# A graph network on one core: four reorderings around the graph stage, the last encoder layer and the decoder's end

## What is computed

```
agg(h) = segment_sum(h[src], dst)                   # the same edges throughout
h = relu(layernorm(x)*g+b @ W1 + b1) @ W2 + b2      # 1024 -> 512 -> 256
3 times: z = relu((h + agg(h)) @ Wa + ba) @ Wb + bb
         h = h + relu(layernorm(z)*g+b)             # encoder, width 256
delta = relu(h @ Wd1 + bd1) @ Wd2 + bd2             # decoder, 256 -> 512 -> 1024
x1 = layernorm(x + layernorm(x + delta)*g+b)
h1 = relu(x1 @ Ws0 + mean(x1) @ Wn0 + b0)           # sage, mean(v) = agg(v)/max(degree,1)
out = layernorm(x1 + h1 @ Ws1 + mean(h1) @ Wn1 + b1)
```

## Time and profile before

| | |
|---|---|
| median of three runs | 1071.99 us (1071.13 to 1073.99) |
| profiled execution, own time | 1074.08 us |
| profiled execution, span | 1072.3 us |
| mean granted clock of TensorE | 0.975 |
| TensorE busy | 1002.2 us, 93% |
| VectorE, ScalarE, GpSimd busy | 536.6, 351.5, 263.8 us |

### The profile page before, as it was taken

One profiled execution on the slowest core, in us unless ns is written; L12 is line 12 of the kernel. 1 busy time (PEld: TensorE's weight loads), 2 busy tenths in 40 slices (PEclk: granted clock), 3 DMA queues, 4 the chain that ended last, 5 costly groups with the idle time before them and its releaser, 6 DMA issues.

```text
span 1072.3 us, 14807 instructions
## 1 busy us (share of the span) xinstructions
PE 1002.2 (93%) x4862; PEld 812.9 (76%) x4862; DVE 536.6 (50%) x1314; ACT 351.5 (33%) x632; POOL 263.8 (25%) x320
## 2 busy tenths in 40 slices
PE   4779899989897898999999999999999999999996
PEld 2367678878787687887777777778887777877774
DVE  7978974374658887333223332222234333334545
ACT  5545552152526477321111221113341011222221
POOL 3000003741416330735004324005206003300000
PEclk9698999999998999999999999999999999999999
DMA  9296344893003584414223104243325335103444
GB/s 327 67 220 186 49 64 89 195 204 84 2 20 109 188 281 150 144 32 138 100 100 102 45 20 160 67 141 128 108 87 166 120 97 164 46 1 121 154 133 133
DMA packets 48263, 127.13 MB, mean 119 GB/s; under 512 B 17775, under 2 KB 18784, under 8 KB 48016
## 3 DMA queue, kind: packets, MB, share of 16 engines
q1 hardware_dynamic: 33622, 74.91, 23.8%
q0 software_dynamic: 8288, 37.29, 12.9%
q10 hardware_dynamic: 6298, 14.21, 3.9%
HBM read 101.76 MB, written 45.13 MB: 137 GB/s over the span
## 4 chain that ended last, share of the span: by engine, by line
PE 83%; DVE 7%; ACT 3%; issue 3%; DMA 2%; POOL 1%; SPq 0%; ACTq 0%; DVEq 0%; POOLq 0%
PE bank L1724 42%; PE bank L1745 17%; PE bank L622 5%; PE bank L1071 5%; PE bank L1103 4%; PE bank L1431 4%; PE bank L586 3%; DMA x_rows<-x 1%; DVE wide L957 1%; PE bank L1412 1%; DVE wide L959 1%; PE bank L1445 1%; ACT xt_f L257 1%; DMA w_f<-W_pairs 1%; PE bank L579 0%
## 5 line engine op out<-in xcount | busy, mean ns | idle before, releaser
L1665 DVE TENSOR_TENSOR h_stage<-h_turned,h_stage 128x1000 fp32r<-128x1000 f32 x80 | 105.5, 1320 | 370.2 <-ACT h_stage L1597 370.2
L1724 PE MATMUL bank<-w_neigh,h_stage 128*125 128x512 f32 x960 | 227.2, 397 | 3.4 <-issue 3.4
L1724 PE MATMUL bank<-w_self,h_stage 128*125 128x512 f32 x960 | 230.3, 395 | 0.0
L1724 PEld LDWEIGHTS bank<-w_neigh,h_stage 128*125 128x125 f32 x960 | 178.2, 187 | 47.3 <-issue 3.6
L1724 PEld LDWEIGHTS bank<-w_self,h_stage 128*125 128x125 f32 x960 | 178.0, 186 | 45.6
L1745 PE MATMUL bank<-g_rows,a_stage 125*125 125x512 f32 x800 | 192.4, 395 | 0.0
L1597 ACT ACTIVATE h_stage<-h_turned 128x1000 fp32r (+1 forms) x80 | 83.8, 1049 | 305.9 <-PE bank L1724 293.5
L1745 PEld LDWEIGHTS bank<-g_rows,a_stage 125*125 125x125 f32 x800 | 148.4, 186 | 37.4
L1562 POOL CAST w_self<-w_stage 128x512 fp32r<-128x512 f32 x32 | 22.7, 711 | 230.2 <-PE bank L1724 221.9
L1103 PE MATMUL bank<-a_turned,gn 125*128 125x418 f32 x360 | 70.5, 354 | 2.8 <-DVE gn L963 2.8
L1103 PEld LDWEIGHTS bank<-a_turned,gn 125*128 125x128 f32 x360 | 67.0, 188 | 4.2 <-DVE gn L963 3.4
(11 more groups left out here) (210 smaller groups left out, 1125.6 us busy)
## 6 DMA issues: line engine op xcount, KB each, us to landing
a_stage<-at_dram SPq DMA_DIRECT2D x40, 625.0 KB, 4.1
w_stage<-w_self POOLq DMA_DIRECT2D x32, 256.0 KB, 3.2
at_dram<-a_turned SPq DMA_DIRECT2D x10, 625.0 KB, 10.5
w_stage<-w_neigh POOLq DMA_DIRECT2D x24, 256.0 KB, 2.9
dec_y<-x_bd SPq DMA_DIRECT2D x10, 512.0 KB, 4.0
dec_x<-x_ob SPq DMA_DIRECT2D x10, 512.0 KB, 4.8
x_dram<-h_rows SPq DMA_DIRECT2D x10, 512.0 KB, 3.0
h_dram<-o ACTq DMA_DIRECT2D x20, 256.0 KB
```

The lines of the kernel that those rows point to most:

```text
L1665: dve.tensor_tensor(st[u][:, 1, :, :], ht[:, :, bass.ds(t * NT, NT)], raw(st[u][:, 0, :, :]), ALU.subtract).then_inc(st_ready, 1)
L1724: mm = pe.matmul(out, st[u][:, a, k, :], w[:, b, k * 512:(k + 1) * 512], start=(k == 0 and p == 0), stop=(k == KD - 1 and p == 2))
```

## The change

1. **Copies of x.** The three pieces are issued in pairs 2, 3 and 4 in place of 0, 1 and 2, still ahead of that pair's `add_eye`.
2. **GpSimd held back.** Before it splits the unit `UNIT_B0` it waits until the degrees are reduced. Behind the layers it waits until all rows of h of the last layer are split, before it forms the low parts of Wd2.
3. **Rows of h.** In the last layer VectorE splits the rows of h of tiles 6 to 9 ahead of the first four products of z1, not behind them.
4. **First h tile.** The decoder's loops end one tile earlier. ScalarE and VectorE do tile 8 in the sage block with the same operations in the same order, except that ScalarE rounds the first tile of h_turned between `roots` and `normalize` of tile 8. `h_stage0` and `h_stage1` change places in memory, so that only the second stage needs the waits for `wn_split` and `x1_read`. TensorE waits for `wn_split` itself.

```diff
@@ -369,8 +369,9 @@
 
         pool.memset(raw(s.at_[:, :, N:NW]), 0.0).then_inc(padded, 1)
         for p in range(PAIRS):
-            own = slice(p * CH, min((p + 1) * CH, N + 128 - NT))
-            for to in ("x_bd", "x_ob") if p < NCH else ():
+            piece = p - (PAIRS - NCH)
+            own = slice(piece * CH, min((piece + 1) * CH, N + 128 - NT))
+            for to in ("x_bd", "x_ob") if piece >= 0 else ():
                 pool.dma_start(io[to][own, :], io["x"][own, :]).then_inc(s.x_copied, 16)
             add_eye(p)
         pool.wait_ge(z1_split, 1)
@@ -830,6 +831,8 @@
 
             if FREED[n]:
                 pool.wait_ge(w_free, FREED[n])
+            if n == UNIT_B0:
+                pool.wait_ge(deg_summed, 1)
             halves(n, SLOT[n])
         pool.wait_ge(s.x_copied, 16 * 2 * NCH)
         for t in range(T):
@@ -837,6 +840,7 @@
                 pool.dma_start(io[to][t * NT:(t + 1) * NT, :], io[row].to_broadcast([NT, D]), accum_op=ALU.add)\
                     .then_inc(x_summed, 16)
         over_layers(pool, layer)
+        pool.wait_ge(h_ready, T * LAYERS)
         for k in range(KH):
 
             hi, lo = [s.w_self[:, h, k * D:(k + 1) * D] for h in range(2)]
@@ -1023,13 +1027,13 @@
             normalize(i, 2)
             for t in range(2, 6):
                 g(t)
-            if last:
-                for j in range(KH):
-                    split_wide(j)
             for t in range(6, T - 1):
                 h_low(dve, i, t)
             g(6)
             h_low(dve, i, T - 1)
+            if last:
+                for j in range(KH):
+                    split_wide(j)
             for t in range(7, T):
                 g(t)
 
@@ -1335,7 +1339,7 @@
             act.sem_inc(x2_out[u], 16)
         act.sem_inc(x2_turned, 2)
         act.wait_ge(const_set, 4)
-        for t in range(T - 1):
+        for t in range(T - 2):
             if t >= 2:
                 fill(act, t - 2)
             deviations(act, t, 0)
@@ -1343,7 +1347,6 @@
             if t >= 1:
                 normalize(act, t - 1)
             deviations(act, t, 1)
-        fill(act, T - 3)
 
     def rstds(dve, t):
 
@@ -1394,13 +1397,13 @@
         rstds(dve, T)
         second_shift(dve, T - 1)
 
-    s.last_rows = last_rows
+    s.decode, s.last_rows = tile, last_rows
 
     @block.vector
     def _(dve):
         dve.sem_inc(x2_ready, 2)
         dve.wait_ge(row_in, 16)
-        for t in range(T - 1):
+        for t in range(T - 2):
             tile(dve, t)
 
     def turn(pe, t):
@@ -1477,7 +1480,7 @@
     f_mv = at("f_mv", [128, 2], F32)
     f_ve, f_rt, f_sc = [at(f"f_{n}", [128, 1], F32) for n in ("ve", "rt", "sc")]
     f_rs, f_sh = [[at(f"f_{n}{u}", [128, 1], F32) for u in range(2)] for n in ("rs", "sh")]
-    assert at.at <= s.st_at[1], at.at - s.st_at[1]
+    assert at.at <= s.st_at[0], at.at - s.st_at[0]
     ps_g, ps_self, ps_t, ps_a = s.banks[2:4], s.banks[0:2], s.banks[4:6], s.banks[6:8]
     HF = T // 2
     OUT_ROWS = ((0, 120), (120, NT))
@@ -1631,11 +1634,17 @@
         act.sem_inc(ht_ready, 1)
         act.sem_inc(f_normed, 4)
         act.sem_inc(h_used, 2)
+        s.fill(act, T - 4)
+        s.deviations(act, T - 2, 0)
+        s.roots(act, T - 2)
         act.wait_ge(s.ht_filled, 4)
+        stage(0, 0, 0)
+        s.normalize(act, T - 3)
+        s.deviations(act, T - 2, 1)
+        s.fill(act, T - 3)
         act.wait_ge(*s.wn_split)
         act.wait_ge(*s.x1_read)
-        for u in range(2):
-            stage(0, 0, u)
+        stage(0, 0, 1)
         s.deviations(act, T - 1, 0)
         s.roots(act, T - 1)
         s.normalize(act, T - 2)
@@ -1698,6 +1707,7 @@
 
         dve.sem_inc(g_lo, 2)
         dve.sem_inc(o_done, 2)
+        s.decode(dve, T - 2)
         for u in range(2):
             stage(0, 0, u)
         s.last_rows(dve)
@@ -1763,6 +1773,7 @@
 
         pe.sem_inc(o_mm, 2)
         pe.wait_ge(s.y_read, 2 * (T - 1))
+        pe.wait_ge(*s.wn_split)
         for u in range(2):
             tile(0, 0, u)
             s.turn_x2(pe, T - 2 + u)
@@ -1812,7 +1823,7 @@
     s.xy = [at(f"dec_y{u}", [128, D], F32) for u in range(2)]
     s.xo = [at("dec_x0", [128, D], F32), dec_x1, at("dec_x2", [128, D], F32)]
     s.dec_z = [at(f"dec_z{u}", [128, D], F32) for u in range(2)]
-    s.st_at = [s.dec_at, at.at]
+    s.st_at = [at.at, s.dec_at]
     s.ht_at = at.at + 2 * KD * NT * 4
     assert s.dec_small_at - s.dec_at >= 2 * KD * NT * 4
     s.ht = nc.alloc_sbuf_tensor_at("h_turned", [128, KD, N], F32, offset=s.ht_at)
```

## The result

The changed kernel takes 1067.92 us (median of 22 runs, 1066.68 to 1071.88), the kernel before 1071.12 in the same comparison (22 runs). The ratio is 0.9965, 95% interval 0.9954 to 0.9977: 3.7 us faster (2.5 to 4.9). The forecast was 1068.5, within 1065.5 to 1072.8.

The account below looks back on a forecast made before the run. TensorE, busy 93% of the span, bounds the kernel; only its early idle times can be won. Terms -3.0 - 1.0 + 0.6 - 0.1 = -3.5 us from 1071.99 give 1068.5 us, range 1065.5 to 1072.8.

Parts of the forecast that it names:

- 1. Copies of x: At the second load of x rows: moving the copies shortens the load, net -3.0 us (-5.0 to -0.5).
- the clock at 0: At TensorE's shortened rest for the x load: the clock still drops, so 0 gained on top, not 1.5 us.
- The cost of the moved copies at the second load: At the x load issued near 100 us: overlap with the moved first piece of copies costs 0.2 us.
- the slack that I had counted: First layer's weights: split by GpSimd 1.8 us before TensorE needs them, so delay by moved copies costs 0.
- a sign of being wrong: At the first layer's weights: being split later than W2's product ends would show the prediction wrong; no size given.
- 2. Degrees: At the degrees' reduction: holding GpSimd's subtraction back frees 1.1 us, taken as -1.0; 0 if the stride sets the time.
- 3. Rows of h: At the last layer's end: VectorE's z1 splits finish later, +0.1 to +1.2 us, taken +0.6; bounds -0.4 to +5.2.
- the clearing shuts out a subtraction: At z1's splits: if GpSimd's clearing doesn't shut out VectorE's subtraction, split 8 and the whole come 0.5 us sooner.
- 4. First h tile: At the decoder-to-sage boundary: first product starts 3.3 us sooner, but TensorE rests before tile 8's turn; stall moved, -0.1 us.
- the reduction isn't held: Rival at the degrees: GpSimd doesn't slow the reduction, so its 1.0 us isn't gained; 1069.5 us, chance 0.22.
- The slower one: Rival at the last layer's end: GpSimd's fourth subtraction bounds, decoder begins 5.2 us later; 1073.1 us, chance 0.12.

Follow-up runs that it names:

- the fastest kernel: Changed kernel with z1's splits between the rows of h, GpSimd's clearing held until z1's split, both first sage products before the last two turns: 1062.87 us, ratio 0.9874.
- second reduction: Changed kernel plus another reduction of the same 1250 elements in memory order, behind the degrees' one; that reduction took 1.43 us, no kernel time given.

## Why the prediction was right, and where it was not

**1. Copies of x: -3.0, measured -4.8 in the pair of traces, -3.7 over all.** The mechanism is right, shown by taking the step back. The load gave 3.57 (I took 3.2). On top TensorE's first product behind the stall took 3.33 where it had taken 4.37 (`84.02 4.37 PE bank L622 x24`), and the first one behind the next load 2.97 for 3.53. I had put the clock at 0 there, and the other kernels bear that out: behind the short load the first product took 2.83 to 4.37, and 3.10 behind the long one of the copies put back. The cost of the moved copies at the second load, 0.2, didn't come: 3.63 against 3.67. Weights weren't late after: GpSimd had split them at 175.29, 1.8 ahead of the end of W2's product (177.09), the slack that I had counted. But that slack doesn't always do. In the fastest kernel the last pair's stores landed 14.5 us behind their issue (154.35 to 168.85; after 11.6), and TensorE rested 1.05 for the weights, one of the things that I had named as a sign of being wrong. It is one of eleven traces with the copies late; that the copies beside the stores did it is likely and not shown.

**2. Degrees: -1.0, measured -0.1. The failed step.** "[S]o held back, the subtraction frees 1.1". The rate of 1.04 ns an element is right (1.45 counted, 1.43 measured), but for ten sums of elements in order; nearly all of the 2.54 is the price of this reduction's own shape, and GpSimd's part in it is 0.08. The other value that I had bounded it by, 0, is close to the true one. The rule that I had cited from the Trainium skill, SBUF — State Buffer, section "Who interferes with whom", that a tensor_reduce never contends, agrees with these traces to within 0.1 us: 2.54 with GpSimd's subtraction beside it, 2.46 and 2.47 without. The wait cost nothing on the chain either. The split it holds ran at 182.45. The load of the next unit comes behind that split, and the next unit's own split began 26.3 us behind W2's product, where before it began 24.2 behind (192.32 - 168.14); that stayed covered, as I had counted:

```profile
182.45 1.04 POOL L800 CAST weight_slots<-w_f 128x1024 fp32r<-128x1024 f32 x1 [7.16 <-DVE degrees L1052]
...
189.71 1.04 POOL L800 CAST weight_slots<-w_f 128x1024 fp32r<-128x1024 f32 x1 [3.73 <-DMA w_f<-w_units]
```

**3. Rows of h: +0.1 to +1.2, taken +0.6.** Counting VectorE was right: the first sum came 1.05 later by W2's product, +1.2 predicted. The timeline after shows the count's parts, TensorE no longer waiting for the rows, but for relus and splits:

```profile
327.65 0.53 DVE L763 TENSOR_TENSOR ht<-h_f,ht 128x250 fp32r<-128x250 f32 x1 [1.99 <-ACT ht L876]
...
328.24 5.98 PE L1075 MATMUL bank<-ht,weight_slots 128*128 128x418 f32 x30 [0.53 <-DVE ht L763]
...
331.80 2.57 DVE L961 CAST wide<-act_out 128x418 fp32r<-128x418 f32 x1
...
335.76 4.00 PE L1075 MATMUL bank<-ht,weight_slots 128*128 128x418 f32 x18 [1.53 <-ACT act_out L866]
...
344.64 4.43 DVE L961 CAST wide<-act_out 128x418 fp32r<-128x418 f32 x1
```

Also right were that GpSimd's wait does nothing in this order, and that the shorter rest ahead of the first turn (1.29) keeps the clock: the turn took 1.07 and the product 5.52, not 1.93 and 6.18. The second turn is 0.47 earlier by W2's product, below my +0.1. What I did not see is that the wait and the order work against each other. With the rows behind, the wait alone is worth 1.7 to 1.9; the new order makes it idle and loses 1.0 more. Whether the clearing shuts out a subtraction, as I had weighed, doesn't show after: it met only casts there, as in the last row above, which ended behind it. The kernel with the rows behind and the wait kept shows that it doesn't; the subtraction in the middle of the clearing took its usual time:

```profile
344.03 2.27 POOL L1284 MEMSET h_rows<- 128x1024 f32 x2
```

```profile
345.43 0.60 DVE L963 TENSOR_TENSOR wide<-act_out,wide 128x418 fp32r<-128x418 f32 x1
```

**4. First h tile: -0.1, measured -0.1 up to the last turn, and -0.5 behind it.** The stall was moved, not removed: the first product follows its turn at 409.79, and TensorE rests 3.00 ahead of the next turn (predicted 3.2). The size is right by two errors that cancel: that turn took 1.07 and its product 7.13, not 1.93 and 6.18. The 0.5 us that sage's products take less in every kernel with this step wasn't in the prediction at all.

**The sum.** By the traces, from W2's product on: +1.05 at the first sum, -0.5 at the last turn, -1.0 at the end. With step 1 at 3.7 that makes -4.7 against the forecast's -3.5 and the timed -3.7 (2.5 to 4.9). The overpriced step 2 (0.9) and the underpriced steps 1, 3 and 4 (0.7, 1.1 and 0.5) made up for each other in part, so that the time came so near the forecast is partly luck. The interval lies on both sides of 0.3%, as the forecast did. Of the rivals, "the reduction isn't held" was true as a mechanism. The slower one, 5.2 us from GpSimd's fourth subtraction, wasn't: wherever GpSimd waited 2.6 us for ScalarE's rounding, VectorE did five or six operations and not one.

## To carry to other kernels

Before you reorder for the engine that idles, find what the next stage's first instruction waits for: here TensorE's 3.8 us of rest was harmless, and filling it took the time from VectorE, which was late. A wait that keeps one engine out of another's way has a worth only in an order in which it binds, so the two are tried in all four combinations. And a stall that sits behind a queue's next item is removed by putting ready work ahead of that item (both products before the turns), not by bringing one product forward.

## What the hardware showed that I had not expected

**The clock after a rest isn't settled by the rest's length.** After a rest of 3.0 us in the same place the product took 7.13 in the changed kernel and 5.59 in the one with the second reduction. TensorE's timeline there, whose rows begin 0.24 earlier than those of the chain, first after, then the other:

```profile
418.56 1.07 PE L1415 MATMUL bank<-ident,h_rows 125*128 125x125 f32 x8 [3.00 <-ACT h_rows L1321]
419.39 7.37 PE L1734 MATMUL bank<-w_neigh,h_stage 128*125 128x512 f32 x24
```

```profile
419.56 1.07 PE L1416 MATMUL bank<-ident,h_rows 125*128 125x125 f32 x8 [2.99 <-ACT h_rows L1322]
420.39 5.83 PE L1735 MATMUL bank<-w_neigh,h_stage 128*125 128x512 f32 x24
```

By windows the granted clock after is 0.76 over 418.5 to 421 and 0.63 over 421 to 424; in the other it is 1.00 throughout. Two of eight kernels with this rest kept the clock (copies back, second reduction). The rest of 1.9 ahead of the degrees' row went the other way: of thirteen kernels, two lost the clock behind it (copies back, 4.55 us; waits out, 4.40; the others 3.0 to 3.2). So 1.5 us of a single trace's difference can be chance, and with such drops at several rests W2's first product varied by 3.4 us between kernels that are the same up to there. What decides stays open.

**The shape of a reduction** cost 1.0 us on 10 partitions x 1250 elements: 2.0 ns an element as 125 sums over a strided axis, 1.1 as ten sums in memory order.
